# A gated cross-attention and mixture-of-experts block: three key blocks of the probabilities added on GpSimd ahead of the ones pass, K regrouped and V loaded per group

## The reference

```python
# x [16, 512, 512]; ctx_2048 [16, 512, 1024]; lengths itok [16, 1]; all float32
x = x + tanh(g_xattn) * xattn(ctx_2048, layernorm(x), b, itok)
x = x + tanh(g_ffn) * ffn(layernorm(x), w1, b1, w2, b2, centroids, w_route)

def xattn(memory, query, b, seq_len):          # 16 heads of 32 columns
    k_mem, v_mem = split(memory, 2, axis=2)
    Q = heads(query) * 32 ** -0.5; K = heads(k_mem); V = heads(v_mem)
    logits = einsum('bhqd,bhkd->bhqk', Q, K) + b
    logits = logits + MASK_VALUE * (1 - valid)  # keys at or past seq_len
    return softmax(logits) @ V                  # per head, 512 x 512 probabilities

def ffn(x, ...):   # 8 experts, top 2 by cosine plus routing scores, 512 -> 256 -> 512, exact gelu
    ...
```

## Time and profile before

| | |
|---|---|
| three runs | 2139.34, 2145.31 (median), 2153.35 us |
| profiled execution | 2141.61 us |
| its span, first to last instruction | 2139.6 us |
| mean granted TensorE clock | 0.955 |

### The profile page before, as it was taken

The page is one execution under the profiler, slowest core; times in us unless marked ns, Lnnn a source line. Parts: engine busy times, 40 slices in busy tenths (PEclk is TensorE's granted clock), DMA queues, the critical chain, the costliest instruction groups (busy, mean ns, idle before and its releaser), DMA issues. The chain is left out here.

```text
span 2139.6 us, 38585 instructions
## 1 busy us (share of the span) xinstructions
PE 1901.1 (89%) x10720; PEld 1060.5 (50%) x10721; DVE 1597.0 (75%) x3742; ACT 1127.1 (53%) x1999; POOL 737.5 (34%) x547
## 2 busy tenths in 40 slices
PE   0599999999999999999999999998399988989887
PEld 0344444444444444444444444443277766767675
DVE  6578788777877878877777787773477777777776
ACT  0166655656556565655655665654155555555554
POOL 1112111111111111211201111100168888888887
PEclk9899999999999999998999999998599999999999
DMA  3878687676867877777777786653358677777674
GB/s 110 141 109 162 117 181 139 133 153 125 179 133 137 178 142 134 162 114 173 142 130 151 126 184 111 140 125 125 98 114 145 135 132 138 149 125 131 131 135 67
DMA packets 173114, 292.01 MB, mean 136 GB/s; under 512 B 37982, under 2 KB 42078, under 8 KB 172944
## 3 DMA queue, kind: packets, MB, share of 16 engines
q1 hardware_dynamic: 140016, 222.26, 51.0%
q0 software_dynamic: 32928, 67.68, 17.8%
HBM read 127.09 MB, written 71.63 MB: 93 GB/s over the span
## 5 line engine op out<-in xcount | busy, mean ns | idle before, releaser
L918 DVE TENSOR_REDUCE mx<-bank 128x1 f32<-128x512 f32 x1024 | 693.8, 687 | 243.6 <-PE bank L714 231.5
L622 ACT ACTIVATE prob<-bank 128x512 f32<-128x512 f32 x1024 | 579.6, 596 | 492.1 <-PE bank L702 491.4
L590 POOL TENSOR_TENSOR regrouped_then_w<-regrouped_then_w 128x512 fp32r<-128x512 f32 x128 | 166.5, 1301 | 1145.9 <-ACT regrouped_then_w L612 1145.9
L714 PE MATMUL bank<-stA,stB 98*128 98x512 f32 x1024 | 428.4, 420 | 67.4 <-DVE mx L918 40.8
L702 PE MATMUL bank<-stB,stA 100*128 100x512 f32 x1024 | 469.2, 460 | 9.8 <-issue 9.5
L702 PEld LDWEIGHTS bank<-stB,stA 100*128 100x128 f32 x1024 | 196.9, 193 | 212.5 <-ACT prob L622 116.3
L675 PE MATMUL bank<-prob,vin 128*32 128x512 f32 x2048 | 279.6, 619 | 0.0
L675 PE MATMUL bank<-prob,ones 128*32 128x512 f32 x2048 | 278.9, 617 | 0.0
L1150 POOL DMA_INDIRECT rows_in<-xn_rows,gather_ids x152 | 221.3, 1456 | 162.7 <-DVE rows_in L1360 121.3
L714 PEld LDWEIGHTS bank<-stA,stB 98*128 98x128 f32 x1024 | 202.8, 198 | 113.2 <-DVE mx L918 73.0
L1180 POOL DMA_INDIRECT out_dram<-yout,scatter_ids x144 | 231.7, 1609 | 39.2 <-issue 30.4
(11 more groups left out here) (182 smaller groups left out, 2095.6 us busy)
## 6 DMA issues: line engine op xcount, KB each, us to landing
stB<-regrouped_then_w SPq DMA_DIRECT2D x192, 256.0 KB, 5.5
stA<-regrouped_then_w SPq DMA_DIRECT2D x192, 256.0 KB, 8.4
x_k_then_w<-in_x_dram SPq DMA_DIRECT2D x16, 1024.0 KB, 6.1
x_k_then_w<-in_ctx_dram SPq DMA_DIRECT2D x16, 1024.0 KB, 8.6
vin<-in_ctx_dram SPq DMA_DIRECT2D x16, 1024.0 KB, 6.4
xres<-in_x_dram SPq DMA_DIRECT2D x16, 1024.0 KB, 12.8
xn_rows<-xn SPq DMA_DIRECT2D x64, 256.0 KB, 2.2
out_dram<-xres SPq DMA_DIRECT2D x16, 1024.0 KB, 10.5
```

What stands on the lines that cost most here:

```text
L590: pool.tensor_tensor(turnedL[:, side, :], turned[:, side, :], turnedH[:, side, :].bitcast(F32), ALU.subtract).then_inc(s_lo, 1)
L622: act.activation(prob[:, u % 2, j, :], psS[j % 2][:, :], ACT.Exp).then_inc(s_exp, 1)
L714: pe.matmul(psM[s % 2][:, :], stB[0:98, g, j, i * P:(i + 1) * P], stA[0:98, g, j, :], start=True, stop=True).then_inc(s_m, 1)
L918: dve.tensor_reduce(mx[:, s // 4, s % 4:s % 4 + 1], psM[s % 2][:, :], AX.X, ALU.max).then_inc(s_mx, 1)
```

## The change

GpSimd adds the probabilities of key blocks 0, 1 and 2 per head, eight adds of 128 x 512 per step, in place in block 0. The ones pass reads this sum and the last block: two sets at slot 2 of the next step in place of four in all. V's sets stay, at slots 5, 9, 13 and 1. `prob` gets four blocks, of which the first two change places from step to step. K is regrouped per group into one of two small buffers, V is loaded per group (256 KB, pieces of 512 bytes), K's load moves to g2, and TK comes before MT (slots 3 and 4), OT is copied before DT. The slots of some VectorE work move by one or two. `attT`, `sumT` and `mT` become single buffers in `w2a`, which changes the order of the weight loads.

```diff
-TURNS = [("TQ", 3), ("XT", -5), ("MT", 1), ("TK", 3), ("DT", -1), ("OT", -1), ("LG", -5)]
+TURNS = [("TQ", 3), ("XT", -5), ("TK", 3), ("MT", 1), ("DT", -1), ("OT", -1), ("LG", -5)]
...
-            vin = sb("vin", [P, 2, NT, D])
+            vin = sb("vin", [P, NG, NT, P])
...
-            prob = sb("prob", [P, 2, HG, S])
+            prob = sb("prob", [P, NT, HG, S])
...
+            PV = NT + 1
+            ADDS = 2 * HG
+
+            def prob_of(st, off, u):
+                return prob[:, u if u >= 2 else (st.l + off + u) % 2, :, :]
...
+                    if st.g() == 2 and st.on(6):
+                        par = ((st.l + 6) // 4) % 2
+                        if st.rnd is not None or st.l >= 2:
+                            sp.wait_ge(s_kg, st.count(1, 2, 0))
+                        b = st.batch(1, 6, 0)
+                        sp.dma_start(kin[:, par, :, :], c_d[bass.ds(b, 1), :, :, 0:D].rearrange("a p i d -> p (a i) d")).then_inc(s_k[par], 16)
+                    if st.on(2):
+                        g = st.g(2)
+                        if st.rnd is not None or st.l >= 2:
+                            sp.wait_ge(s_pv, st.count(PV, -2, NT))
+                        b = st.batch(1, 2, 0)
+                        sp.dma_start(vin[:, g, :, :], c_d[bass.ds(b, 1), :, :, D + g * P:D + (g + 1) * P].rearrange("a p i d -> p (a i) d")).then_inc(s_v[g], 16)
...
+                    if st.on(0):
+                        first, more, then = [prob_of(st, 0, u) for u in range(3)]
+                        pool.wait_ge(s_pv, st.count(PV, 0, 1))
+                        for j in range(HG):
+                            pool.wait_ge(s_exp, st.count(16, 0, HG + j + 1))
+                            pool.tensor_tensor(first[:, j, :], first[:, j, :], more[:, j, :], ALU.add).then_inc(s_acc, 1)
+                        for j in range(HG):
+                            pool.wait_ge(s_exp, st.count(16, 0, 2 * HG + j + 1))
+                            pool.wait_ge(s_acc, st.count(ADDS, 0, j + 1))
+                            pool.tensor_tensor(first[:, j, :], first[:, j, :], then[:, j, :], ALU.add).then_inc(s_acc, 1)
...
-                        pool.tensor_copy(kg[:, :, :].rearrange("p i (g c h) -> p (i g) h c", g=NG, h=HG),
-                                         kin[:, kpar, :, :].rearrange("p i (g h c) -> p (i g) h c", g=NG, h=HG)).then_inc(s_kg, 1)
+                        pool.tensor_copy(kg[:, st.l % 2, :, :].rearrange("p i (c h) -> p i h c", h=HG),
+                                         kin[:, kpar, :, g * P:(g + 1) * P].rearrange("p i (h c) -> p i h c", h=HG)).then_inc(s_kg, 1)
...
-                                act.wait_ge(s_pv, st.count(8, 0, 2 * u - 2))
+                                act.wait_ge(s_pv, st.count(PV, -1, (2, PV, 3, PV)[u]))
+                                if u in (0, 2):
+                                    act.wait_ge(s_acc, st.count(ADDS, -1, ADDS if u else HG))
...
+                def sums(st, off):
+                    pe.wait_ge(s_acc, st.count(ADDS, off, ADDS))
+                    if st.rnd is not None or st.l + off >= 1:
+                        pe.wait_ge(s_out, st.count(2, off, 0))
+                    for u in (0, NT - 1):
+                        p = prob_of(st, off, u)
+                        for j in range(HG):
+                            last = pe.matmul(psD[DH * j:DH * (j + 1), :], ones[:, 0:DH], p[:, j, :],
+                                             start=(u == 0), stop=(u > 0), skip_group_check=True,
+                                             tile_position=(0, DH * j))
+                    last.then_inc(s_pv, 1)
...
+                        if j == 1 and u > 0 and st.on(0):
+                            values(st, 0, u - 1)
+                        if s == 1 and st.on(-1):
+                            values(st, -1, NT - 1)
+                        if s == 2 and st.on(-1):
+                            sums(st, -1)
...
-                        if st.g() == 0 and 1 <= s <= 4 and st.on(4):
-                            normalise_q(st, s - 1)
+                        if st.g() == 0 and s in (1, 3, 5, 7) and st.on(4):
+                            normalise_q(st, s // 2)
...
-                        if st.g() in (1, 2) and s in (6, 11) and st.on(8 - st.g()):
-                            stats(st, 2 * (st.g() - 1) + s // 11)
+                        if st.g() in (1, 2) and s in (3, 13) and st.on(8 - st.g()):
+                            stats(st, 2 * (st.g() - 1) + s // 13)
```

More of the change, by code:

```diff
@@ L407, in flamingo_kernel @@
             s_k = [sem(f"k_loaded{i}") for i in range(2)]
-            s_v = [sem(f"v_loaded{i}") for i in range(2)]
+            s_v = [sem(f"v_loaded{i}") for i in range(NG)]
             s_res = [sem(f"residual_loaded{i}") for i in range(2)]
@@ L522, in step @@
                         place_rows(stB, 0, g, 1, turnedH)
-                    if st.on(1):
-                        i, before = turn_of(st, "MT")
-                        sp.wait_ge(s_took[i], before + 1)
-                        for t in range(2):
-                            sp.dma_start(stB[98 + t:99 + t, st.g(1), :, :].bitcast(F32), mT[HG * t:HG * t + HG, :].bitcast(F32)).then_inc(s_md[(st.l + 1) % 2], 16)
                     if st.on(3):
@@ L536, in step @@
                         place_rows(stA, 1, g, 2, turnedH)
+                    if st.on(1):
+                        i, before = turn_of(st, "MT")
+                        sp.wait_ge(s_took[i], before + 1)
+                        for t in range(2):
+                            sp.dma_start(stB[98 + t:99 + t, st.g(1), :, :].bitcast(F32), mT[HG * t:HG * t + HG, :].bitcast(F32)).then_inc(s_md[(st.l + 1) % 2], 16)
+                    if st.on(3):
                         sp.wait_ge(s_lo, st.count(2, 3, 2))
-                        place_rows(stA, 1, g, 1, turnedL)
+                        place_rows(stA, 1, st.g(3), 1, turnedL)
                     if st.g() == 1 and st.on(-5):
@@ L557, in step @@
                                      gates[:, par, :, :]).then_inc(s_gst[par], 16)
[L558 to L561 removed]
+                    if st.rnd is None and 0 <= st.l - (G - 4) < E // 2:
+                        if st.l == G - 4:
                             sp.wait_ge(s_xg, B)
[L563 to L564 removed]
+                            sp.wait_ge(s_kg, G)
+                        for e in range(2 * (st.l - (G - 4)), 2 * (st.l - (G - 4)) + 2):
+                            sp.dma_start(w1_all[:, e, :, :], w1[e].rearrange("(k p) n -> p k n", p=P)).then_inc(s_w, 16)
                     if st.rnd is None and 0 <= st.l - (G - 2) < E // 2:
@@ L569, in step @@
                                 sp.wait_ge(s_stk[side], 48 * G)
-                        for e in range(2 * (st.l - (G - 2)), 2 * (st.l - (G - 2)) + 2):
+                        if st.l == G + 1:
+                            for name in ("DT", "OT"):
+                                i, before = turn_of(st, name, -1)
+                                sp.wait_ge(s_turn[i], before + 1)
+                        for e in ((0, 1), (4, 5), (6, 2), (3, 7))[st.l - (G - 2)]:
                             sp.dma_start(w2_all[:, e, :, :], w2[e].rearrange("(k p) n -> p k n", p=P)).then_inc(s_w, 16)
@@ L948, in step @@
                             route_logit(st, s)
-                        if s == 9 and st.on(-1):
+                        if s == 10 and st.on(-1):
                             column_stats(st)
```

111 lines of the change are left out of this document (44 added, 67 removed).

## The result

The changed kernel took 2256.9 us in the median (2249.23 to 2272.58), the kernel before 2142.7 on the same chip (2139.34 to 2153.35), four runs each: ratio 1.054, 95% interval 1.049 to 1.058. It is 114 us slower. The forecast was 2238, with a range of 2005 to 2340. The profiled execution took 2262.5 us, its span is 2260.7.

What follows compares the result with a forecast made beforehand. TensorE was taken to bound light attention steps. Afterwards VectorE's late reduces and holds by GpSimd's adds give 23.6 us per step against 22.07: +95 us over 62 steps, less 3 at the start, about 2238 us; range 2005 to 2340.

Steps and rivals of the forecast that it cites:

- TensorE's floor, 20.25 to 17.8: Attention step: with fewer ones sets, TensorE's own time per step falls from 20.25 to 17.8 us.
- The adds, 1.25 each: GpSimd in each attention step: eight adds of 1.25 us, 10 us in all, some 13.6 us of work per step.
- VectorE's slots 6 to 12 need 7.0 for 6.2; slot 13 is late: VectorE needs 7.0 us there, TensorE 6.2; slot 13's max matmul waits, making the step 19.0 us without holds.
- What the adds hold: VectorE instructions wait for GpSimd's running add: light step (g2) 19.8 us, g3 24.9, g0 25.2, g1 23.5.
- The sum: Four steps 93.4 us plus 1.0 for the loop's edge: 23.6 per step against 22.07, +95 us over 62 steps, less 3.
- The time: Whole kernel: about 2238 us forecast after the change.
- Little is held, 2014: Rival: adds hold little of VectorE's work; 19.95 us per step, -131 us, 2014; chance 0.28 with part held.
- Neighbours go together: Rival: consecutive VectorE instructions keep the shared port and wait once, not each; +16 us, 2160; chance 0.20.
- Port kept: Rival: GpSimd keeps the shared port from add to add; 25.1 us per step at least, 2350 and more; chance 0.14.
- The clock: Rival: TensorE's waits in g3 and g0 bring half clock, adding 90 us: 2330; no separate chance given.
- Given back: Attention stage: the 3.91 us K copy, its 3.4 hold and 1.84 wait in g0 go; transfers priced at nothing.

## Why the prediction was right

**TensorE's floor, 20.25 to 17.8.** The matmuls went as counted (16 records per step). The floor was not reached in the loop: with one-column adds and the statistics early the shortest step there is 18.2, the mean 21.06.

**The adds, 1.25 each.** 1.28 in the median, and up to 1.72 where VectorE's residual add gets in between. GpSimd was to be busy about 70% of the stage; 13.6 of 23.6 us, the forecast's own terms, are 58%, and 455.35 of 762.84, 60%, were measured.

**VectorE's slots 6 to 12 need 7.0 for 6.2; slot 13 is late.** Shown: the wait stands at slot 13 (1.40 us at 688.13 with one-column adds) and its clock cost goes when 0.8 us of VectorE's work leaves these slots. For g2 19.0 had been worked out without holds; with one-column adds and the clock full it took 19.4 to 19.5 inside the loop (cut at `nm`). What the late slot costs was mis-sized: the step without holds is 21.91 in the mean, not 19.95, for the clock falls behind such waits.

**What the adds hold.** Right in kind: held to the end of the running add, first to go at it, next one held again (L974, L127). g2 was put at 19.8: cut at `nm`, most of those at full clock took 19.7, the mean is 20.3; cut at the first logits matmul, as in the forecast, 19.7 to 20.3 at full clock. But its parts were off in both directions, and that the step fits is luck: without holds it takes 19.4 and not 19.0, and the holds lengthen it by 0.3 and not 0.8. In the medians L974 is held 0.3 us, the residual add 0.6, the logits sum 0.2, where 0.6, 0.7 and 0.4 had been put. g3 at 24.9: 24.79 in the step shown, 25.1 in the mean. g0 and g1, with the loop's edge, at 25.2 + 23.5 + 1.0 = 49.7: 27.7 + 21.6 = 49.3, cut at `nm`. TensorE waits for row maxima 83 times in the 32 steps, where it did 14 times. The Trainium skill, SBUF — State Buffer, "Who interferes with whom", would have the residual add held, of which the trace before showed nothing: the trace agrees, 1.27 us in the median, 0.68 with one-column adds; and so for the logits sum, 0.41 and 0.22.

**The sum.** 23.6 per step was forecast, 23.84 measured. Two errors lie in it that cancel, which is luck. Clock loss was left out of the four steps (a rival had it, at 90 us), and there is some in g3, g0 and g1 (0.88, 0.86, 0.90); so at a full clock the holds alone cost less than I made of them. How much of the 23.84 is clock can only be bounded: 0.87 granted means about 0.26 of the time at 1.2 GHz, for 0.06 before, so at most half of 0.2 x 762.84 us was lost, 76 us or 2.4 per step; the extra idle time of TensorE is 1.5 (78.2 us idle for 31.2, over 32 steps). The kernel with one-column adds and early statistics has the same matmuls at a clock of 0.97 and is busy with them 626.09 us for 684.68, 1.8 per step less.

**The time.** 2257 for 2238, 19 us short. +0.24 per step too little is 15 of it, and the 3 us gained at the start do not show: the first gather comes 117.7 us later than before, the forecast had 92. It stood on a kernel before of 2145.3; against the 2142.7 measured beside it the change costs 114 us.

**The rivals.** *Little is held, 2014*: not this kernel, and its price was wrong. The kernel that tests it would, by its first stage, be about 11 us faster than before, not 131. The range's low end was too low by the same error. *Neighbours go together*: no; L974 and L127 follow one another and each waits. *Port kept*: it exists, in 1 or 2 of 64 steps of three other kernels, at up to 7.0 us, and in none of this one; I gave it 0.14 as an all-or-nothing case. The Trainium skill, GPSIMD Engine Reference, "Instruction dispatch", has each core begin its next instruction when its own share of the last is done, which I had taken as speaking for this rival; the traces have it as the exception. *The clock*: part of the outcome, not an alternative to it.

**Given back.** The long K copy's hold and the batch's transfers: the kernel with all but the adds is 0.3 us per step faster than before, which is the worth of it. Transfers stayed covered, as priced: TensorE waits for none in the 32 steps. With the steps of 21.06 they begin to show, 10.4 us in 32 steps.

## What to carry to other kernels

Work for an idle GpSimd is not free while VectorE has many small SBUF instructions: count these, not their time, since each that falls beside a GpSimd instruction waits for its end, and the next one begins in step with the next. Eight unread adds cost 4% here, a part of it by pushing a long copy to where it did more harm. Before a pass is taken from TensorE, put the engine that feeds it through the same slots; when that becomes the bound, TensorE's waits cost its clock as well, and half a saving can come out as nothing. When a chain is moved, look at what then falls at the step's end.

## What I had not expected of the hardware

Shorter holders do not shorten the wait in proportion: with GpSimd adds of 0.7 us in place of 1.28, a 16-element product took 0.75 us in the median in place of 0.54, while the residual add fell from 1.27 to 0.86; VectorE's busy time in the 32 steps fell by 5 us of the 86 that are holding.

A waiting VectorE instruction mostly goes first when a GpSimd instruction ends, but not always: one residual add waited 6.17 us past the ends of four adds, one `nm` took 2.41 us, past a copy's end and through the subtraction behind it. Nothing in the rows tells these cases from the others; what decides between them stays open. The holding goes both ways: an add of 1.28 us took 1.71 beside the residual add.

TensorE's clock: the same matmuls took 651 us with waits for the maxima of up to 1.4 us, and 626 us with none above 0.9, at an idle time that was nearly the same.
